# A graph layer on one core: GpSimd waits for landed rows at every half tile, two context chunks behind the chain, feed-forward weights loaded later

## The chip, the cores and the metric

The kernel runs on one core of one Trainium2 chip. The time is the device time of one execution, in microseconds (us); lower is better. TensorE is called PE in the profile, VectorE DVE, ScalarE ACT, GpSimd POOL and SyncE SP.

## The reference

The input is a table `x` of 6250 nodes with 256 channels, and 106,250 edges (source, target), sorted by target. Every node is normalized (layer norm) to `xn`. Then three things are computed and added up:

```python
# graph attention, 4 heads of 64 channels
h = (xn @ W).reshape(-1, 4, 64)
e = leaky_relu(a_src[src] + a_dst[dst], 0.2)      # a_src, a_dst: h times a vector per head
ex = exp(e - segment_max(e, dst)[dst])
alpha = ex / segment_sum(ex, dst)[dst]
gat = sigmoid(segment_sum(alpha * h[src], dst) + bias)
# linear attention over all nodes, 8 heads, with a gate
q, k, v = split(xn @ Wqkv); k = softmax(k, axis=nodes)
context = einsum(k, v); out = q @ context
mix = (out * sigmoid(gelu(ln(xn) @ Wg1 + bg1) @ Wg2 + bg2)) @ Wproj + bproj
x = x + gat + mix
# feed-forward on the nodes that a top-k of a router weight selects
y = (gelu(ln(x) @ w1 + b1) @ w2 + b2) * weight    # zero where not selected
x = x + y + ln(x)
```

## The kernel before, in words

Nodes are cut in 49 tiles of 128 rows (`NT`), edges in 52 tiles of 2048 (`NI`). Every engine has its own program; the programs meet at semaphores. The program has a setup block, a block for a fallback that isn't entered with these inputs, the main block, and a short last block that writes the result.

The **setup block** (from L250) loads all of `x`, takes the means and variances (DVE, `stats`, L427), forms the inverse root (L483 to L503), multiplies every node tile by the weights (PE, L674 and L680) and stores per node a row of 260 numbers (`feat_d`, 256 channels and the source scores) and smaller rows of target scores (`adst_d`). DVE moves the products out of PE's accumulator (`evacuate`, L514 to L530), SP stores them (L302). In between GpSimd and DVE prepare the edge lists: DVE casts them to float (L462), GpSimd works on them (L354 to L406). SP also loads the two feed-forward weights there (L330, 1 MB each), into space that the edge lists held until then.

The **main block** handles edge tile k in these stages. GpSimd fetches the source rows: 16 indirect DMAs (`gather`, L737) of 128 rows each, in 4 groups of 4 (`fill`). They land in `ring`, which has a slot for even k and one for odd k, and each group counts up a semaphore of its own (`rows_in{u}{g}`, u the slot, g the group). A group of tile k may only be issued once PE has summed the half of tile k-2 that held its place (`sums_done`). The scores of the edges go PE (L1552), DVE (L1178 to L1198), PE (turned, L1568), DVE (two scans that form the running maxima, L1206 and L1209), PE (turned back, L1577), DVE (L1218, L1222), ACT (exponentials, L1425). Then DVE scales the gathered rows (L1235, one operation per group) and PE sums them by target (L1610, 8 products a group), and ACT copies each half's sums out (L1444), after which GpSimd may reuse that half.

The other work of a step belongs to node tiles some steps behind: merging the sums (5 behind), the linear attention's products and the gate (6 behind; PE L1531, L1539, L1621; ACT L1455; DVE L1135), the feed-forward's first product (7 behind, L1638, GELU on ACT L1472) and its second (L1589, taken out by DVE L1228, 8 behind). `steps(engine, list)` lays the stages of one step out in the order of the list, for every engine apart, so the lists in the last lines of each engine's program set the order. Steps 0 to 9 and the last ones are written out, the others are a loop of two steps.

The **context** of the linear attention sums over all nodes, so it must be done before the first merge. It is cut in 10 chunks (`CHUNKS`): chunk 0 stands ahead of step 0, and the steps 0 to 4 hold the other nine. Each needs loads of `x` by SP (L1055), DVE, ACT (L1406, L1414) and PE (L1488).

```python
        CONTEXT_A = lambda f: (0, 5, lambda k, u: f(2 * k + 1, u))
        CONTEXT_B = lambda f: (0, 4, lambda k, u: f(2 * k + 2, u))
                        pool.wait_ge(S("idx_made"), 2)
```

`known_below(k, n)` is true where k is a constant under n; `number` turns a step's number into what the engine compares with. `sweep` is a loop over tiles with a body of `n` tiles.

## Time and profile before

| | us |
|---|---|
| median of 3 runs | 2220.82 (2220.32 to 2227.02) |
| the profiled execution's own time | 2227.13 |
| its span, first to last instruction | 2225.3 |
| PE busy | 1179.6 |
| DVE busy | 1046.6 |
| POOL busy | 835.9 |
| ACT busy | 570.4 |
| mean granted TensorE clock | 0.71 |

The span is what the trace covers. Busy is the time in which an engine executed; time in which it waited for a semaphore or issued a DMA is not in it. No engine is busy for much more than half of the span, so what matters is which wait ends last in each stretch. In the rows further down, the idle time of an engine ahead of an instruction stands in brackets with what released it: an engine, a value and a line, or `issue`, which is time in which the engine waited for nothing that the profile shows, or `remote`, a wait whose releaser can't be named from the records.

### The profile page before, as it was taken

To read this page: it belongs to the slowest core of one execution; us is meant where nothing else is said; L and a number is where in the kernel's file an instruction comes from. 1 tells how busy PE (TensorE), PEld (TensorE's weight loads), DVE (VectorE), ACT (ScalarE), POOL (GpSimd) and SP (SyncE) were. 2 spreads that over 40 slices of the span, in tenths; PEclk is the share of its full clock that TensorE was granted. 3 is DMA by queue.
4 is the path that set the end of the run, shared out by engine and by line. 5 is a ranking of instruction groups with operands and counts; after the bars stand their busy time and mean duration, and the time that the engine had idled before them with its cause. 6 is when DMAs were issued, how large, how long until landed. Compare 5 with 4: busy or idle time off the path is not lost. (4 is left out here: it accounts for less than half of the span.)

```text
span 2225.3 us, 26752 instructions
## 1 busy us (share of the span) xinstructions
PE 1179.6 (53%) x6583; PEld 925.9 (42%) x6583; DVE 1046.6 (47%) x2649; ACT 570.4 (26%) x1372; POOL 835.9 (38%) x881
## 2 busy tenths in 40 slices
PE   4975344544545455454545464646363636364682
PEld 3753223323434444343434353535352525343571
DVE  7543334353544444444535353535353535353557
ACT  3432211111222222222222222313131313131360
POOL 4002342444434343535353535353434343444200
PEclk7987666666767676767677667667667767676795
DMA  6566342333333332323232323232323333333203
GB/s 172 184 165 169 96 114 81 87 99 100 89 82 91 78 94 75 98 71 97 72 100 71 103 66 103 71 98 76 93 74 95 79 95 78 93 85 86 70 22 116
DMA packets 166018, 210.85 MB, mean 95 GB/s; under 512 B 51163, under 2 KB 130587, under 8 KB 165871
## 3 DMA queue, kind: packets, MB, share of 16 engines
q0 software_dynamic: 39984, 110.94, 19.7%
q1 hardware_dynamic: 125991, 99.41, 15.8%
q8 instruction: 18, 0.29, 0.1%
q14 instruction: 25, 0.20, 0.0%
HBM read 165.93 MB, written 44.30 MB: 94 GB/s over the span
## 5 line engine op out<-in xcount | busy, mean ns | idle before, releaser
L737 POOL DMA_INDIRECT ring<-feat_d,idx x832 | 801.1, 963 | 1122.0 <-issue 569.6
L1638 PE MATMUL bank<-late,w_s 128*128 128x128 f32 x1568 | 312.9, 382 | 659.9 <-ACT late L1465 659.9
L1638 PEld LDWEIGHTS bank<-late,w_s 128*128 128x128 f32 x1568 | 304.6, 293 | 690.1 <-issue 630.6
L1228 DVE TENSOR_TENSOR big<-bank,b2row 128x256 f32 (+1 forms) x49 | 20.8, 424 | 592.2 <-remote 592.0
L1610 PE MATMUL bank<-ring,hot 128*64 128x265 f32 x1664 | 217.7, 414 | 49.0 <-DVE ring L1235 45.1
L1235 DVE TENSOR_TENSOR ring<-ring,bank 128x1024 f32<-128x1024 f32 x208 | 240.0, 1217 | 1.8 <-ACT bank L1425 1.8
L1455 ACT ACTIVATE sc<-bank,hbg 128x128 f32<-128x128 f32 x98 | 30.6, 363 | 816.9 <-remote 806.2
L1589 PE MATMUL bank<-w_s,hT 128*128 128x256 f32 x784 | 185.9, 390 | 3.7 <-ACT hT L1472 3.7
L1610 PEld LDWEIGHTS bank<-ring,hot 128*64 128x64 f32 x1664 | 125.4, 145 | 124.0 <-issue 68.3
L1589 PEld LDWEIGHTS bank<-w_s,hT 128*128 128x128 f32 x784 | 146.9, 193 | 22.7 <-ACT hT L1472 4.3
L1472 ACT ACTIVATE hT<-bank,b_s 128x128 f32<-128x128 f32 x392 | 110.3, 372 | 44.8 <-PE bank L1638 44.2
L1488 PE MATMUL bank<-big,sc 128*128 (+1 forms) x196 | 71.2, 516 | 89.3 <-issue 43.3
L1488 PEld LDWEIGHTS bank<-big,sc 128*128 128x128 f32 x196 | 45.9, 252 | 112.1 <-issue 95.5
L1568 PE MATMUL bank<-ident,lk 128*16 128x128 f32 x208 | 37.9, 299 | 100.6 <-issue 68.0
L1425 ACT ACTIVATE bank<-diff 128x64 f32<-128x64 f32 x52 | 11.8, 228 | 305.6 <-DVE diff L1222 298.5
L1621 PE MATMUL bank<-wproj_s,sc 128*128 128x256 f32 x196 | 86.2, 585 | 0.0
L1444 ACT ACTIVATE wout<-bank 128x265 f32<-128x265 f32 x104 | 40.7, 392 | 169.8 <-PE bank L1610 167.7
L1089 DVE TENSOR_TENSOR late<-late,big 128x256 f32<-128x256 f32 x49 | 20.8, 425 | 118.0 <-ACT big L1406 59.8
L1218 DVE TENSOR_TENSOR ring<-bank,lastT 128x64 f32<-128x64 f32 x52 | 11.7, 225 | 119.7 <-PE bank L1577 106.3
L674 PE MATMUL bank<-late,xnT 128*128 128x328 f32 x196 | 66.5, 464 | 0.6 <-ACT xnT L592 0.6
L1206 DVE TENSOR_TENSOR_SCAN forth<-brk,bank 16x512 f32<-16x512 f32 x52 | 62.5, 1202 | 8.9 <-PE bank L1568 6.2
L1153 DVE TENSOR_TENSOR hot<-bank,dlocT 128x512 f32<-128x512 f32 x104 | 66.5, 680 | 0.0
(249 smaller groups left out, 1729.8 us busy)
## 6 DMA issues: line engine op xcount, KB each, us to landing
parts_d<-wout SPq DMA_DIRECT2D x208, 66.2 KB
ring<-feat_d,idx POOLq DMA_INDIRECT x832
lists<-dloc_d SPq DMA_DIRECT2D x104, 128.0 KB
parts_d<-hot SPq DMA_DIRECT2D x50, 265.0 KB
parts<-parts_d SPq DMA_DIRECT2D x49, 265.0 KB
xs<-in_x SPq DMA_DIRECT2D x74, 128.0 KB
feat_d<-parts SPq DMA_DIRECT2D x49, 130.0 KB, 2.9
big<-in_x SPq DMA_DIRECT2D x7, 896.0 KB, 10.8
```

What stands on the lines that cost most here:

```text
L674: mm = T.matmul(bank[2 + u][:, 0:WA], tile[:, t * P:(t + 1) * P], wa_s[:, t, :], start=(t == 0), stop=(t == CT - 1))
L737: pool.indirect_dma_start(out=ring[:, u * TI + q, 0:AW], out_offset=None, in_=feat_d, in_offset=bass.IndirectOffsetOnAxis(ap=idx[:, u, q:q ...
L1153: V.tensor_tensor(hot[:, tiles, :], iota_ps.unsqueeze(1).to_broadcast([P, 2 * TG, WIN]), dlocT[:, bass.ds(k, 1), tiles].rearrange("p a q - ...
L1206: V.tensor_tensor_scan(forth[:, :], brk[:, 0:GE], bk_t[0:TI, :], LOWEST, ALU.add, ALU.max).then_inc(S("forth_made"), 1)
L1235: V.tensor_tensor(feats, feats, ex[:, g * TG:(g + 1) * TG, :].unsqueeze(3) .to_broadcast([P, TG, HEADS, HD]), ALU.mult).then_inc(S("scaled ...
L1444: A.activation(wout[:, n, :], bank[2 + n][:, 0:SW], ACT.Copy).then_inc(S("sums_kept"), 1)
L1472: A.activation(hT[:, m, :], bank[6 + m // 4][:, (m % 4) * P:(m % 4 + 1) * P], ACT.Gelu_apprx_tanh, bias=b1_s[:, m:m + 1]).then_inc(S("gelu ...
L1488: mm = T.matmul(bk_c[t][:, 0:C], sc[:, u, t * P:(t + 1) * P], big[:, bass.ds(i, 1), :].rearrange("p a c -> p (a c)"), start=s, stop=e)
L1589: mm = T.matmul(bk_o[:, 0:C], hT[:, m, :], w2_s[:, m, :], start=(m == 0), stop=(m == FT - 1))
L1610: mm = T.matmul(bank[2 + n][c * WIN:(c + 1) * WIN, 0:SW], hot[:, q, :], ring[:, u * TI + q, 0:SW], start=(j == 0), stop=(j == TG - 1))
L1621: mm = T.matmul(bk_t[:, 0:C], sc[:, u, t * P:(t + 1) * P], wproj_s[:, t, :], start=(t == 0), stop=(t == CT - 1))
L1638: mm = T.matmul(bank[6 + m // 4][:, (m % 4) * P:(m % 4 + 1) * P], w1_s[:, t, m * P:(m + 1) * P], xn2T[:, t * P:(t + 1) * P], start=(t == 0 ...
```

## The change

Four things are changed.

1. GpSimd's `fill` waits for rows to have landed. Ahead of group 2 of a tile it waits until groups 0 and 1 of this tile are there, ahead of group 0 (from tile 1 on) until group 3 of the tile before is there. Four groups make a tile, so there are never more than 8 indirect DMAs under way.
2. The two context stages of a step stand together, late in the step, on SP, DVE, ACT and PE; before, one of them stood at the head of the step. Each engine's list has one entry fewer.
3. SP loads the two feed-forward weights at the head of the main block, ahead of `steps`, instead of in the setup block, whose end then doesn't wait for them. PE waits for them ahead of its first feed-forward product.
4. DVE casts the edge lists behind the first four `evacuate`, instead of between two parts of the statistics.

```diff
@@ setup block, SP @@
                 store_targets(1)
-                sp.wait_ge(S("lists_turned"), 6)
-                sp.wait_ge(S("order_checked"), 1)
-                for o, i in later:
-                    sp.dma_start(o, i).then_inc(S("ffn_in"), 16)
                 sweep(sp, TARGETS[2], NT, 0, 0, store)
...
-                sp.wait_ge(S("ffn_in"), 32)
@@ setup block, DVE @@
                 stats(4)
-                dve.wait_ge(S("edges_in"), 32)
-                for n, to in enumerate((ed_dst, ed_src)):
-                    V.tensor_copy(to, ed_i[:, (1 - n) * IE:(2 - n) * IE]).then_inc(S("edges_float"), 1)
                 stats(5)
...
-                sweep(dve, 0, STOPS[1], 2, 0, evacuate)
+                for i in range(4):
+                    evacuate(i, i % 2)
+                dve.wait_ge(S("edges_in"), 32)
+                for n, to in enumerate((ed_dst, ed_src)):
+                    V.tensor_copy(to, ed_i[:, (1 - n) * IE:(2 - n) * IE]).then_inc(S("edges_float"), 1)
+                sweep(dve, 4, STOPS[1], 0, 0, evacuate)
@@ the context's place @@
-        CONTEXT_A = lambda f: (0, 5, lambda k, u: f(2 * k + 1, u))
-        CONTEXT_B = lambda f: (0, 4, lambda k, u: f(2 * k + 2, u))
+
+        def CONTEXT(f):
+
+            def two(k, u):
+                for n in range(2 * k + 1, min(2 * k + 3, len(CHUNKS))):
+                    f(n, u)
+
+            return 0, 5, two
+
@@ main block, GpSimd @@
-                        made, used = number(pool, k + 1), None
+                        made, used, landed = number(pool, k + 1), None, None
                         if not known_below(k, 2):
                             used = number(pool, NB * (k - 2) + g // 2 + 1)
+                        if g == 2:
+                            landed = (f"rows_in{u}{g - 1}", number(pool, 32 * (k - u) + 64))
+                        elif g == 0 and not known_below(k, 1):
+                            landed = (f"rows_in{1 - u}{GI - 1}", number(pool, 32 * (k - 1 - (1 - u)) + 64))
                         pool.wait_ge(S("idx_made"), 2)
                         if g == 0:
                             pool.wait_ge(S("idx_made"), made)
+                        if landed is not None:
+                            pool.wait_ge(S(landed[0]), landed[1])
                         if used is not None:
                             pool.wait_ge(S("sums_done"), used)
@@ main block, SP @@
+                for o, i in later:
+                    sp.dma_start(o, i).then_inc(S("ffn_in"), 16)
+
-                steps(sp, [CONTEXT_A(context), AHEAD(ahead), MERGE(load_x), CONTEXT_B(context), AHEAD(breaks_ahead),
+                steps(sp, [AHEAD(ahead), MERGE(load_x), CONTEXT(context), AHEAD(breaks_ahead),
                            EDGES(windows), NODE_AHEAD(load_node)])
@@ main block, PE @@
                 def first_ff1(i, u):
                     pe.wait_ge(S("xn2T_kept"), i + 1)
+                    if known_below(i, 1):
+                        pe.wait_ge(S("ffn_in"), 32)
                     ff1_half(i, 0)
...
-                steps(pe, [CONTEXT_A(context), EDGES(turn_scores), FF1(first_ff1), EDGES(turn_maxima), SUM(project), FF1(other_ff1),
-                           EDGES(first_sums), EDGES(other_sums), AHEAD(scores_ahead), CONTEXT_B(context), FF1(ff2),
+                steps(pe, [EDGES(turn_scores), FF1(first_ff1), EDGES(turn_maxima), SUM(project), FF1(other_ff1),
+                           EDGES(first_sums), EDGES(other_sums), AHEAD(scores_ahead), CONTEXT(context), FF1(ff2),
                            FOLD(fold), MERGE(mixer), SUM(turn_normed), SEARCH(search)])
```

The lists of DVE and ACT change in the same way. What this makes of the order is shown at three places. The line numbers of the changed kernel differ a little (L737 is L734 there).

GpSimd, tile 1's last group and tile 2's first three. A row with a wait is the first gather of a group, "x3" the other three. Before:

```order
L737 DMA ring<-feat_d,idx 128x260 [waits idx_made]
L737 DMA ring<-feat_d,idx 128x260 x3
L737 DMA ring<-feat_d,idx 128x260 [waits sums_done,idx_made]
L737 DMA ring<-feat_d,idx 128x260 x3
L737 DMA ring<-feat_d,idx 128x260 [waits sums_done,idx_made]
L737 DMA ring<-feat_d,idx 128x260 x3
L737 DMA ring<-feat_d,idx 128x260 [waits sums_done,idx_made]
```

And of the change:

```order
L734 DMA ring<-feat_d,idx 128x260 [waits idx_made]
L734 DMA ring<-feat_d,idx 128x260 x3
L734 DMA ring<-feat_d,idx 128x260 [waits rows_in13,sums_done,idx_made]
L734 DMA ring<-feat_d,idx 128x260 x3
L734 DMA ring<-feat_d,idx 128x260 [waits sums_done,idx_made]
L734 DMA ring<-feat_d,idx 128x260 x3
L734 DMA ring<-feat_d,idx 128x260 [waits sums_done,rows_in01,idx_made]
```

Every other group has one more wait. No gather has moved.

SP's queue at the head of the main block: the loads of `x` for context chunks (L1055, L1065), two weights, then the target scores (`stat`) for the next edge tile. Before:

```order
L1004 DMA brk<-brk_d 16x512
L1055 DMA xs<-in_x 128x256 [waits renormed] x2
L1055 DMA sa<-in_x 128x256 [waits renormed] x2
L1069 DMA hT<-in_L0_mix_Wqkv 128x2x256
L1070 DMA parts<-in_L0_mix_Wqkv 128x2x256
L1055 DMA xs<-in_x 128x256 [waits renormed] x2
L1055 DMA sa<-in_x 128x256 [waits renormed] x2
L975 TENSOR_LOAD base_i
L998 ISA
L998 DMA stat<-adst_d 64x12
```

And of the change:

```order
L1014 DMA brk<-brk_d 16x512
L1065 DMA xs<-in_x 128x256 [waits renormed] x2
L1065 DMA sa<-in_x 128x256 [waits renormed] x2
L1079 DMA hT<-in_L0_mix_Wqkv 128x2x256
L1080 DMA parts<-in_L0_mix_Wqkv 128x2x256
L1084 DMA w1_s<-in_L0_ffn_w1 128x2x1024
L1084 DMA w2_s<-in_L0_ffn_w2 128x8x256
L985 TENSOR_LOAD base_i
L1008 ISA
L1008 DMA stat<-adst_d 64x12
```

The two weights (1 MB each) stand where the loads for chunk 1 stood, and those loads come behind the target scores.

PE, the start of step 0. `stat` and `lists` give the edges' scores, `sc` and `big` are the context's factors, `lk` the scores, `srow` the maxima. Before:

```order
L1552 MATMUL bank<-stat,lists 128x24 x7
L57 UNCONDITIONAL_BRANCH
L57 ISA
L1488 ISA [waits renormed,keys_exp]
L1488 MATMUL bank<-big,sc 128x256 x2
L1484 REGISTER_ALU
L1488 ISA [waits renormed,keys_exp]
L1488 MATMUL bank<-big,sc 128x256 x2
L57 REGISTER_ALU
L57 COMPARE_AND_BRANCH
L1568 MATMUL bank<-ident,lk 16x128 [waits leaky_made]
L1568 MATMUL bank<-ident,lk 16x128 x3
```

And of the change:

```order
L1565 MATMUL bank<-stat,lists 128x24 x7
L1581 MATMUL bank<-ident,lk 16x128 [waits leaky_made]
L1581 MATMUL bank<-ident,lk 16x128 x3
L1590 MATMUL bank<-ident,srow 128x16 [waits max_made,idx_made]
L1590 MATMUL bank<-ident,srow 128x16 x3
L1623 MATMUL bank<-ring,hot 64x265 [waits hot_made,ex_made,scaled,maxcol_made,lastcol_made]
```

The context chunk's products have left the place ahead of the step's chain; they follow behind the scores of the next tile.

## Rows read from the trace of the kernel before

**Rows 1.** The page's busy times of the engines, whole span.

```profile
PE 1179.6 (53%) x6583; PEld 925.9 (42%) x6583; DVE 1046.6 (47%) x2649; ACT 570.4 (26%) x1372; POOL 835.9 (38%) x881
```

**Rows 2.** The page's costliest groups: busy, mean ns of one, idle before and its releaser.

```profile
L737 POOL DMA_INDIRECT ring<-feat_d,idx x832 | 801.1, 963 | 1122.0 <-issue 569.6
...
L1228 DVE TENSOR_TENSOR big<-bank,b2row 128x256 f32 (+1 forms) x49 | 20.8, 424 | 592.2 <-remote 592.0
...
L1455 ACT ACTIVATE sc<-bank,hbg 128x128 f32<-128x128 f32 x98 | 30.6, 363 | 816.9 <-remote 806.2
```

**Rows 3.** Timeline of one loop step: start, duration (us), engine, line, operation, [idle before].

```profile
1002.22 0.94 POOL L737 DMA_INDIRECT ring<-feat_d,idx  x1 [17.45 <-issue]
...
1003.13 3.70 PE L1589 MATMUL bank<-w_s,hT 128*128 128x256 f32 x16
...
1007.65 0.71 PE L1539 MATMUL bank<-hidT,wg_s 64*128 64x128 f32 x4
...
1010.15 0.61 PE L1568 MATMUL bank<-ident,lk 128*16 128x128 f32 x4 [1.42 <-issue]
...
1021.30 0.95 POOL L737 DMA_INDIRECT ring<-feat_d,idx  x1 [0.30 <-issue]
1025.52 0.42 DVE L1228 TENSOR_TENSOR big<-bank,b2row 128x256 f32 x1 [15.43 <-remote]
1025.57 0.62 ACT L1455 ACTIVATE sc<-bank,hbg 128x128 f32<-128x128 f32 x2 [18.89 <-remote]
...
1030.61 0.66 PE L1577 MATMUL bank<-ident,srow 16*128 16x16 f32 x4
...
1031.40 0.23 DVE L1218 TENSOR_TENSOR ring<-bank,lastT 128x64 f32<-128x64 f32 x1 [2.39 <-PE bank L1577]
...
1032.36 4.62 DVE L1235 TENSOR_TENSOR ring<-ring,bank 128x1024 f32<-128x1024 f32 x4
...
1036.59 3.80 PE L1610 MATMUL bank<-ring,hot 128*64 128x265 f32 x32
...
1038.79 0.39 ACT L1444 ACTIVATE wout<-bank 128x265 f32<-128x265 f32 x1 [0.94 <-PE bank L1610]
...
1039.62 0.95 POOL L737 DMA_INDIRECT ring<-feat_d,idx  x1 [17.38 <-PE bank L1610]
```

**Rows 4.** DMA engines' busy tenths in 40 slices, window 1023.5 to 1024.5 us.

```profile
DMA  8800400000000000000000000000000000000000
```

**Rows 5.** Group of L1218 from 600 to 2000 us: first and last start.

```profile
L1218 DVE TENSOR_TENSOR ring<-bank,lastT x38: 224/226/226, 628.1 to 1984.6; 128x64 f32<-128x64 f32 x38
```

**Rows 6.** Timeline of the setup block where the feed-forward weights load.

```profile
170.43 1.36 SPq L330 DMA_DIRECT2D w_s<-in_L_ffn_w  x2
...
187.06 0.49 DVE L514 TENSOR_SCALAR parts<-bank,rstd 128x260 f32<-128x260 f32 x1 [14.09 <-DMA feat_d<-parts]
```

**Rows 7.** Timeline of the setup block around casts and the inverse root.

```profile
28.02 2.35 DVE L462 CAST w_s<-ring 52x2048 f32<-52x2048 int32 x2
...
40.37 5.37 POOL L360 TENSOR_SCALAR ring<-ring 52x2047 f32<-52x2047 f32 x1
...
40.66 3.41 DVE L489 TENSOR_TENSOR xs<-rstd 128x49 f32<-128x49 f32 x1
...
52.65 0.36 DVE L489 TENSOR_TENSOR xs<-rstd 128x49 f32<-128x49 f32 x1
```

**Rows 8.** Timeline of the main phase's first steps, GpSimd and ScalarE.

```profile
205.23 0.95 POOL L737 DMA_INDIRECT ring<-feat_d,idx  x1 [41.15 <-POOLq L760]
...
244.43 0.95 POOL L737 DMA_INDIRECT ring<-feat_d,idx  x1 [0.30 <-issue]
...
250.55 0.60 ACT L1414 ACTIVATE sc<-xs,rstd_neg,rstd 128x256 f32<-128x256 f32 x1 [9.06 <-remote]
...
273.50 0.95 POOL L737 DMA_INDIRECT ring<-feat_d,idx  x1 [28.13 <-PE bank L1610]
...
312.40 0.94 POOL L737 DMA_INDIRECT ring<-feat_d,idx  x1 [18.61 <-PE bank L1610]
```

More of the change, by code:

```diff
@@ L1396, in _ @@
                 context(0, 0)
-                steps(dve, [CONTEXT_A(context), EDGES(target_scores), EDGES(edge_hots), EDGES(scores), OUT(outputs),
+                steps(dve, [EDGES(target_scores), EDGES(edge_hots), EDGES(scores), OUT(outputs),
                             SUM(products), EDGES(maxima), EDGES(differences), MERGE(merge_weights), EDGES(messages), AHEAD(hots_ahead),
-                            CONTEXT_B(context), SUM(sums), MERGE(merge), SUM(normed), FOLD(fold), SEARCH(search)])
+                            CONTEXT(context), SUM(sums), MERGE(merge), SUM(normed), FOLD(fold), SEARCH(search)])
             @block.scalar
@@ L1476, in _ @@
                 context(0, 0)
-                steps(act, [CONTEXT_A(context), EDGES(exps), MERGE(merge_exp), GELU(hidden), EDGES(keep_sums), CONTEXT_B(context),
+                steps(act, [EDGES(exps), MERGE(merge_exp), GELU(hidden), EDGES(keep_sums), CONTEXT(context),
                             SUM(inverse_root), MERGE(gates), SUM(keep_turned)])
```

## The prediction

> **What bounds the kernel now.** I read the page first. GpSimd's 832 gathers fill only 801.1 us of a 2225.3 us span; PE is the busiest engine with 53% [rows 1, 2]. So nothing is at its limit, and I looked at the waits. Two groups stand out: DVE's L1228 is preceded by 592.2 us of idle time and ACT's L1455 by 816.9 us, nearly all of it "remote" [rows 2]. Both wait for a product of PE in every step.
>
> The timeline of one loop step shows why [rows 3]. The step goes from the first gather at 1002.22 to the next tile's first gather at 1039.62: 37.4 us. The gathers start at 1002.22 and follow each other by 1.27 us; the sixteenth starts at 1021.30 and ends at 1022.25, so the train takes 20.0 us. PE's L1589 is finished at 1003.13 + 3.70 = 1006.83, and its reader L1228 starts at 1025.52. PE's L1539 is finished at 1007.65 + 0.71 = 1008.36, and its reader L1455 starts at 1025.57. Both readers start together, 17 to 19 us after their inputs were ready and 3.3 us after the last gather's end. DVE itself can't be the reason: before L1228 it idled 15.43 us; nor ACT, which idled 18.89. My reading: **what PE reports is held while GpSimd issues gathers, and comes out some 3.3 us after the train**. L1568, the turned scores, ended at 1010.76 and is read only behind L1228.
>
> After the release comes the chain that GpSimd waits for: from L1228 (1025.52) 5.09 us to L1577, 0.79 to L1218, 0.96 to L1235 (4.62 us for four groups), the sums L1610, their copy L1444 at 1038.79, and 0.83 us later the next gather. Release to next train: 14.1 us. Train start to release: 23.3. A step is the sum of these two, since the train of tile k+2 needs the sums of tile k and these need the release behind the train of tile k+1. L1218 starts at 628.1 and, 37 intervals later, at 1984.6: 36.66 us a step in the mean [rows 5].
>
> **The waits for landed rows.** They add two pauses to a step, one in the middle and one ahead of the next tile. How long does GpSimd pause? Around the end of a train the DMA engines work until the slice that ends at 1023.63 at most [rows 4] (the fifth slice of 0.025 us behind 1023.5), some 1.4 us after the last gather's end at 1022.25. A restart on a semaphore takes up to 0.83 us, as after L1444 [rows 3]. Landing (1.4, up to 1.7 with the semaphore itself) plus restart: 2.2 to 2.5 us; I take 2.5. Ahead of a tile this costs nothing, for there GpSimd waits 17.38 us for the sums [rows 3]; rows landed long before. In the middle it counts: the train becomes two halves of 7 x 1.27 + 0.95 = 9.85 us with 2.5 us between them, 22.2 us instead of 20.0.
>
> The Trainium skill, "DMA: Bandwidth & Descriptors", section "Anatomy of one DMA — SWDGE (gpsimd) path", gives such a DMA a fixed cost of about 2.0 us, most of it the confirmation that the last byte has landed, ahead of the semaphore. By it a middle pause would be some 0.5 us longer than by the row, 52 x 0.5 = 26 us in the sum; it speaks against a wait for landing, as this change adds one.
>
> What the pause may give back: if what PE reports is let out when GpSimd stands still with nothing under way, the products of the first half step (L1589, L1539, L1568) reach their readers about 3.0 us after the first half, at 9.85 + 3.0 = 12.9 us from the train's start, not at 23.3. DVE and ACT then do L1228, L1455 and the scans during the second half. L1577 follows 5.1 us later, at 18.0: that lies inside the second half (12.4 to 22.2), so its report is held again until 22.2 + 3.3 = 25.5. Then L1218 at once; L1235 0.96 later, two groups of it 2.3; 16 of the sums' products 1.9 (half of 3.80); copy and restart 0.9. Next train at 25.5 + 0.96 + 2.3 + 1.9 + 0.9 = 31.6, 31.7 with rounding up of the parts. Before, PE was busy with a product of the feed-forward when L1235's first groups were ready (L1610 starts at 1036.59, 4.2 us after L1235); that product now lies earlier. Against the mean of 36.7 this is 5.0 us a step. Steps 8 to 51 are 44: **-220 us**. Bounds: from -11.6 a step (no hold left, below) to +2.5 a step (no release in the pause).
>
> **The weights' load.** In the setup, SP issues the two loads of 1 MB at 170.43, and the `feat_d` stores behind them come late: DVE waits 14.09 us for such a store before its evacuation at 187.06 [rows 6]. This goes: -14. In the main block the loads stand ahead of the target scores of tile 1, where only chunk 1's loads stood. There their 2 MB take the time that they took in the setup, 12 to 14 us, and what covers it is step 0, whose gathers alone run 39 us [rows 8]; if that cover is gone, +12, once. I take 0.
>
> **The casts.** They take 2.35 us [rows 7], and GpSimd's preparation of lists starts with them. In before it runs beside DVE's inverse root: L489 takes 3.41 us beside GpSimd's L360 and 0.36 us without it. The root's chain has five such stretches, together some 8.5 us, an estimate from this pair. The change runs the root alone, but puts the casts (2.35) and the slow stretches among the first evacuations, where DVE has slack. I take -4, half of it; bounds -8.5 and +2.4.
>
> The Trainium skill, "SBUF — State Buffer", section "SBUF: two separate sides", says that a DVE operation with two inputs in SBUF and a GpSimd operation lock each other out; by this rule, the trace agrees, with 3.41 against 0.36 us.
>
> **The context behind the chain.** The first train is of two tiles, 32 gathers from 205.23 to 245.38 [rows 8]; ACT's next context operation starts at 250.55, after 9.06 us of "remote", 5.2 us behind the train. Steps 1 and following take 38.9 us there (273.50 to 312.40). The order now lets the edge tile's chain go first, and chunk loads wait less in the way of the scores. The five steps could each win up to the chunk's products and the wait ahead of them, some 8 us, as much as the 9.06 us wait; and with the pauses above the steps 0 to 7 gain like the loop. But the context must be done before the first merge, and its two chunks a step remain. I take -30 for steps 0 to 7 in all; bounds 0 and -58 (8 x 7.3).
>
> **Sum.** 2227.13 - 220 - 14 - 4 - 30 = 1959 us for an execution like the profiled one. Its own time lies 6.3 us over the median of the runs, so I forecast 1950 (rounded from 1953).
>
> **Rivals.**
>
> *B: no hold at all with at most 8 gathers under way.* If the hold needs a long train (it shows itself behind 16 and 32 gathers; nothing shows 8), all of PE's reports come promptly. Then a step is bounded by GpSimd: 2 x (9.85 + 2.5) and 0.4 for small pauses, 25.1 us, since the chain of 14.1 us and the 8.5 us ahead of it (1002.22 to 1010.76) are 22.6 together. 44 x (25.1 - 36.7) = -510; 2227 - 510 - 48 = 1669, to 1750 if half of the second half's hold is left. For it: reports that end before the train aren't held. Against: L1539 was finished 6 us into the train, with 5 gathers issued, and was held already.
>
> *C: slower.* The release came 3.3 us after the last gather, the pause lasts only 2.5. If what lets reports out is the end of work that runs on for 3.3 us (5.2 behind 32 gathers, so it grows with the train), the second half begins before anything has been let out, and the hold runs through both halves. Then nothing is gained and every tile pays the 2.5 us: 52 x 2.5 = +130, less the 18 of the setup: 2227 + 130 - 18 = 2339, or 2300 with the context's gain. The point from which it decides: whether the tail behind 8 gathers is shorter than 2.5 us. Going from 5.2 for 32 to 3.3 for 16, 8 would leave 2.3, just under it. That makes this the strongest rival.
>
> *D: the release in the pause happens, but wins little,* since the chain's end stays behind the second half and ACT and DVE have other work there: -1 to -2 us a step, 2100 to 2200.
>
> *E: the waits find the rows landed, no pause, no gain.* Against: a group's last gather is issued 0.3 us ahead of the wait, its rows land 1.4 us later [rows 3, 4]. Only setup and context would count then, and if they also come to nothing, it is the same.
>
> **Chances.** Forecast 0.50, own range 1830 to 2090 (-3 to -9 us a step). B 0.12. D 0.08. E with nothing 0.03. C 0.27. So faster by over 0.3% 0.70, within 0.3% 0.03, slower 0.27; 0.3% (7 us) is about what a measurement of this kernel can tell from no change. The range goes from 1780, which leaves B out with its 0.12, to 2330, which takes C's likely end in and leaves its tail.
>
> **What would show it.** Right: L737's idle time grows by about 52 middle pauses of 2.5 us, L1228 and L1455 start in or just behind the pause, about 12.9 us after a tile's first gather, their remote waits fall below 400 us, and L1218 comes every 31 to 32 us. B: L1577 is read within 1 us and the pitch is 25 us. C: L1228 starts 25 to 26 us after the first gather, and the pitch of L1218 is 39. Setup: the 14.09 us wait is gone, the main block starts some 18 us earlier. Wrong I would be above all if the release isn't tied to gathers under way, but to something that a pause of 2.5 us doesn't touch.

## The result and the profile after

The changed kernel takes **1705.53 us** (median of 4 runs, 1688.08 to 1724.12) against 2223.7 us for the kernel before in the same set of runs (2220.32 to 2227.02): a ratio of 0.7644, 95% interval 0.7579 to 0.7708. It takes 23.6% less time there. The prediction was 1950 us with a range of 1780 to 2330, so the time lies below the range. The profiled execution of the changed kernel took 1724.12 us, 1.1% over the median; it counts as a slow one and is left out of the ratio, which is that of the means of the others.

And this is only half of the result. On three other chips the kernel before took not 2223 but 1413 to 1415 us, and there the same change makes it 20.7% slower. The experiments below show both.

These rows of the changed kernel's page answer to [rows 1] and [rows 2] (busy time and share, then busy, mean ns of one, idle before and its releaser):

```profile
PE 1185.9 (69%) x6583; PEld 921.9 (54%) x6583; DVE 1041.1 (60%) x2649; ACT 569.1 (33%) x1372; POOL 847.6 (49%) x881
...
L734 POOL DMA_INDIRECT ring<-feat_d,idx x832 | 811.8, 976 | 631.1 <-issue 453.4
...
L1468 ACT ACTIVATE sc<-bank,hbg 128x128 f32<-128x128 f32 x98 | 30.5, 362 | 306.5 <-remote 293.5
...
L1241 DVE TENSOR_TENSOR big<-bank,b2row 128x256 f32 (+1 forms) x49 | 20.7, 423 | 113.2 <-remote 112.3
```

L1228 is L1241 now, L1455 is L1468. The remote wait of the one has gone from 592.0 to 112.3 us, of the other from 806.2 to 293.5. GpSimd's idle time has gone from 1122.0 to 631.1.

One step in the loop, as in [rows 3] (start, duration, engine, line, idle before):

```profile
1008.48 1.15 POOL L734 DMA_INDIRECT ring<-feat_d,idx  x1 [4.21 <-issue]
...
1009.85 3.70 PE L1602 MATMUL bank<-w_s,hT 128*128 128x256 f32 x16
...
1014.38 0.71 PE L1552 MATMUL bank<-hidT,wg_s 64*128 64x128 f32 x4
...
1017.65 0.95 POOL L734 DMA_INDIRECT ring<-feat_d,idx  x1 [0.30 <-issue]
...
1020.47 0.42 DVE L1241 TENSOR_TENSOR big<-bank,b2row 128x256 f32 x1 [3.69 <-remote]
1020.52 0.62 ACT L1468 ACTIVATE sc<-bank,hbg 128x128 f32<-128x128 f32 x2 [7.12 <-remote]
...
1021.39 0.94 POOL L734 DMA_INDIRECT ring<-feat_d,idx  x1 [2.79 <-issue]
...
1025.56 0.66 PE L1590 MATMUL bank<-ident,srow 16*128 16x16 f32 x4
...
1030.13 0.95 POOL L734 DMA_INDIRECT ring<-feat_d,idx  x1 [0.30 <-issue]
1030.28 0.23 DVE L1231 TENSOR_TENSOR ring<-bank,lastT 128x64 f32<-128x64 f32 x1 [6.32 <-remote]
...
1037.40 0.98 POOL L734 DMA_INDIRECT ring<-feat_d,idx  x1 [6.32 <-PE bank L1623]
```

The first half of the tile begins at 1008.48. L1602 and L1552 are finished at 1013.55 and 1015.09, and their readers start at 1020.47 and 1020.52: 12.0 us after the first gather and 1.9 us after the eighth ended (1018.60), while GpSimd pauses. The pause is 2.79 us long. L1590 is finished at 1026.22, when four gathers of the second half have ended, and read at 1030.28: 4.1 us late, but while the train is still running. This step (tile 30) is one of the longer ones, 28.92 us to the next tile's first gather at 1037.40. In tile 42 the second half begins at 1343.29:

```profile
1343.29 0.94 POOL L734 DMA_INDIRECT ring<-feat_d,idx  x1 [2.79 <-issue]
...
1347.38 0.66 PE L1590 MATMUL bank<-ident,srow 16*128 16x16 f32 x4
1348.17 0.23 DVE L1231 TENSOR_TENSOR ring<-bank,lastT 128x64 f32<-128x64 f32 x1 [2.39 <-issue]
...
1355.96 0.94 POOL L734 DMA_INDIRECT ring<-feat_d,idx  x1 [2.96 <-PE bank L1623]
```

Here L1590 is finished at 1348.04, again four gathers into the half, and read at once, at 1348.17. Of the 36 tiles from 12 to 47, 16 are like this one (read within 0.25 us); in the other 20 it is read 0.8 to 5.7 us late, and in 2 of these only when the train has ended. The mean is 19.1 us after the tile's first gather. The 16 steps take 26.1 us in the mean, the 20 others 27.8. The earlier the product was finished, the less it was held: all seven that were finished within 4.52 us of the half's first gather were read at once, the three that came later than 5.0 us were all held.

The pitch of the steps, as in [rows 5]:

```profile
L1231 DVE TENSOR_TENSOR ring<-bank,lastT x22: 224/225/226, 615.4 to 1185.6; 128x64 f32<-128x64 f32 x22
```

(1185.6 - 615.4) / 21 = 27.15 us a step, against 36.66 before. The first gather of all and that of tile 8, from which on the forecast counted its 44 steps:

```profile
186.73 0.95 POOL L734 DMA_INDIRECT ring<-feat_d,idx  x1 [32.39 <-POOLq L757]
...
415.58 0.94 POOL L734 DMA_INDIRECT ring<-feat_d,idx  x1 [2.93 <-issue]
```

The first gather stood at 205.23 before [rows 8], so the setup is 18.5 us shorter. The 1306.7 us from tile 8's first gather to the end of the span, and the 228.9 us between the two, hold the rest of the 503 us: the trace before has its tile 8 at 494.61, which makes 1730.7 and 289.4. So 424 us come from the loop and the end, 60.5 from steps 0 to 7, 18.5 from the setup.

### The profile page after: what moved, and what is told of

Its sections match the earlier page's. It is cut to its first block and busy times, and to the rows that moved or that the text cites. A ratio compares the mean times of both kernels' runs of the same rounds, so it can differ in the third digit from the quotient of the medians.

```text
span 1722.3 us, 26791 instructions
## 1 busy us (share of the span) xinstructions
PE 1185.9 (69%) x6583; PEld 921.9 (54%) x6583; DVE 1041.1 (60%) x2649; ACT 569.1 (33%) x1372; POOL 847.6 (49%) x881
## 5 line engine op out<-in xcount | busy, mean ns | idle before, releaser
L734 POOL DMA_INDIRECT ring<-feat_d,idx x832 | 811.8, 976 | 631.1 <-issue 453.4
L1651 PE MATMUL bank<-late,w_s 128*128 128x128 f32 x1568 | 293.1, 365 | 168.3 <-ACT late L1478 166.2
L1651 PEld LDWEIGHTS bank<-late,w_s 128*128 128x128 f32 x1568 | 284.7, 277 | 189.2 <-issue 175.5
L1623 PE MATMUL bank<-ring,hot 128*64 128x265 f32 x1664 | 253.1, 456 | 97.5 <-issue 52.3
L1623 PEld LDWEIGHTS bank<-ring,hot 128*64 128x64 f32 x1664 | 145.7, 161 | 189.5 <-issue 131.2
L1602 PE MATMUL bank<-w_s,hT 128*128 128x256 f32 x784 | 189.6, 393 | 9.0 <-issue 4.9
L1602 PEld LDWEIGHTS bank<-w_s,hT 128*128 128x128 f32 x784 | 147.8, 194 | 30.4 <-issue 7.4
L1468 ACT ACTIVATE sc<-bank,hbg 128x128 f32<-128x128 f32 x98 | 30.5, 362 | 306.5 <-remote 293.5
L1231 DVE TENSOR_TENSOR ring<-bank,lastT 128x64 f32<-128x64 f32 x52 | 11.7, 225 | 162.8 <-remote 83.7
L1501 PE MATMUL bank<-big,sc 128*128 (+1 forms) x196 | 66.3, 493 | 35.2 <-ACT big L1419 19.3
L1241 DVE TENSOR_TENSOR big<-bank,b2row 128x256 f32 (+1 forms) x49 | 20.7, 423 | 113.2 <-remote 112.3
L1283 DVE TENSOR_SCALAR late<-sd,bn 128x256 f32<-128x256 f32 x49 | 21.1, 431 | 102.1 <-issue 54.2
L1581 PEld LDWEIGHTS bank<-ident,lk 128*16 128x16 f32 x208 | 15.8, 96 | 111.9 <-issue 94.5
L1634 PE MATMUL bank<-wproj_s,sc 128*128 128x256 f32 x196 | 74.3, 515 | 0.0
```

The costliest lines, as they stand in the source:

```text
L734: pool.indirect_dma_start(out=ring[:, u * TI + q, 0:AW], out_offset=None, in_=feat_d, in_offset=bass.IndirectOffsetOnAxis(ap=idx[:, u, q:q ...
L1501: mm = T.matmul(bk_c[t][:, 0:C], sc[:, u, t * P:(t + 1) * P], big[:, bass.ds(i, 1), :].rearrange("p a c -> p (a c)"), start=s, stop=e)
L1581: mm = T.transpose(bk_t[0:TI, :].rearrange("r (e j) -> r j e", j=TG)[:, j, :], lk[:, u, j, :], ident[:, :])
L1602: mm = T.matmul(bk_o[:, 0:C], hT[:, m, :], w2_s[:, m, :], start=(m == 0), stop=(m == FT - 1))
L1623: mm = T.matmul(bank[2 + n][c * WIN:(c + 1) * WIN, 0:SW], hot[:, q, :], ring[:, u * TI + q, 0:SW], start=(j == 0), stop=(j == TG - 1))
L1634: mm = T.matmul(bk_t[:, 0:C], sc[:, u, t * P:(t + 1) * P], wproj_s[:, t, :], start=(t == 0), stop=(t == CT - 1))
```

## The experiments

They ran in five sets, each with the kernel before beside it on the same chip. In four sets, on three chips, the kernel before took 1412.65, 1414.67, 1414.73 and 1415.45 us. In the fourth one in order of time, on another chip, it took 2241.91 us, like the 2223.7 of the result. Nothing lies between. I call the second kind a chip **with the hold**. The expectations of the first set were written before this was known, so they are all made for a kernel before at 2223 us.

### The waits alone, and the change without them (no hold)

e1 is the kernel before with part 1 of the change and nothing else.

```diff
+                        if g == 2:
+                            landed = (f"rows_in{u}{g - 1}", number(pool, 32 * (k - u) + 64))
+                        elif g == 0 and not known_below(k, 1):
+                            landed = (f"rows_in{1 - u}{GI - 1}", number(pool, 32 * (k - 1 - (1 - u)) + 64))
...
+                        if landed is not None:
+                            pool.wait_ge(S(landed[0]), landed[1])
```

> The kernel before with nothing but GpSimd's waits for landed rows. Pause theory (PE's reports are held while gathers are issued without a break, and come out in a pause of some 2 us): nearly the whole gain, 1770 to 1810 us, L1218 every 27 to 28 us in the loop. If setup and context carried it: over 2100 us.

Measured: 1721.17 us, ratio 1.2176 (1.2112 to 1.2240) to the kernel before at 1412.65. The number lies 49 us under the expected range, and it is a loss, not a gain.

e2 is the changed kernel without these lines.

```diff
-                        if g == 2:
-                            landed = (f"rows_in{u}{g - 1}", number(pool, 32 * (k - u) + 64))
-                        elif g == 0 and not known_below(k, 1):
-                            landed = (f"rows_in{1 - u}{GI - 1}", number(pool, 32 * (k - 1 - (1 - u)) + 64))
```

> The changed kernel without its waits for landed rows (other three parts kept). Pause theory: the loop keeps its 36.7 us a step, only setup (-18) and some of the context's steps (up to -30) are gained: 2170 to 2205 us. If the order of context and loads carried the gain: near 1705 us.

Measured: 1391.54 us, ratio 0.9851 (0.9806 to 0.9895). Neither theory had this. The three other parts win 21 us, and the waits cost 314 us (against the change itself, e6, on another chip of the same kind).

### Other spacings (no hold)

e3 waits ahead of every group:

```diff
-                        if g == 2:
+                        if g > 0:
```

> The changed kernel with a wait ahead of every group of 4 gathers. Pause theory: the hold is shorter, but GpSimd's own time is 4 x (3 x 1.25 + 0.95 + 3.0) = 31 us a step, so it becomes the bound: 31 to 32 us a step, 1870 to 1900 us. If fewer gathers under way simply make everything faster: below 1705 us.

Measured: 1949.09 us, ratio 1.3801 (1.3739 to 1.3863), 31.4 us a step as worked out for a GpSimd that is the bound (here 4 pauses of 2.7 to 3.7 us), but in all 49 us over the expected range. The gain that would have paid for it wasn't there to be had.

e4 waits for the group before last only:

```diff
-                        if g == 2:
-                            landed = (f"rows_in{u}{g - 1}", number(pool, 32 * (k - u) + 64))
-                        elif g == 0 and not known_below(k, 1):
-                            landed = (f"rows_in{1 - u}{GI - 1}", number(pool, 32 * (k - 1 - (1 - u)) + 64))
+                        if g > 1:
+                            landed = (f"rows_in{u}{g - 2}", number(pool, 32 * (k - u) + 64))
+                        elif not known_below(k, 1):
+                            landed = (f"rows_in{1 - u}{GI - 2 + g}", number(pool, 32 * (k - 1 - (1 - u)) + 64))
```

> The changed kernel, but a group waits only for the rows of the group before last: never more than 8 gathers under way, as in the change, yet no pause, since those rows land some 1.5 us behind their gather. Pause theory: as without waits, 2170 to 2205 us. If the number under way is what counts: 1640 to 1710 us.

Measured: 1394.20 us, the same as e2 and neither of the two expected. The cap on the gathers under way costs nothing (its trace has 0.30 us ahead of a gather in mid-tile, no pause): it is the standstill that costs.

### The two kernels themselves on such a chip

> The kernel before itself, with a trace. In the runs of the waits alone it took 1412.65 us, where the profiled execution that the prediction reads took 2227. Theory of two modes (the hold of PE's reports is a property of the chip or of how the program sits on it, not of the program): either near 1412 us with L1218 every 20 to 21 us and L1228 within 1 us of PE's product, or near 2223 us with 36.7 us a step, and nothing in between. Theory of a gradual influence (temperature, clock): something in between.

Measured: 1414.81 us, as the theory of two modes says; nothing in between was seen in this set or in any other. Its page (engines, granted clock in tenths of full speed by slices of the span, two groups):

```profile
PE 1064.9 (75%) x6583; PEld 834.2 (59%) x6583; DVE 1052.9 (75%) x2649; ACT 567.6 (40%) x1372; POOL 851.6 (60%) x881
...
PEclk9797968987699999999999999989999998999975
...
L737 POOL DMA_INDIRECT ring<-feat_d,idx x832 | 816.8, 982 | 313.5 <-issue 244.9
...
L1455 ACT ACTIVATE sc<-bank,hbg 128x128 f32<-128x128 f32 x98 | 30.7, 364 | 83.7 <-PE bank L1539 83.7
```

PE is busy for somewhat less than before (1064.9 us against 1179.6 [rows 1], at a higher granted clock), but ACT's L1455 waits 83.7 us in all where it was 806.2 us [rows 2], and the wait has PE's product as its releaser. One step of it:

```profile
899.82 3.70 PE L1589 MATMUL bank<-w_s,hT 128*128 128x256 f32 x16
...
904.35 0.71 PE L1539 MATMUL bank<-hidT,wg_s 64*128 64x128 f32 x4
...
905.09 0.63 ACT L1455 ACTIVATE sc<-bank,hbg 128x128 f32<-128x128 f32 x2 [1.71 <-PE bank L1539]
...
907.74 0.17 DVE L1189 COPY idx<-srcT 128x16 int32 x1 [1.02 <-DMA ring<-feat_d,idx]
...
912.36 0.62 PE L1577 MATMUL bank<-ident,srow 16*128 16x16 f32 x4
...
913.11 0.23 DVE L1218 TENSOR_TENSOR ring<-bank,lastT 128x64 f32<-128x64 f32 x1 [0.90 <-PE bank L1577]
```

L1589 and L1539 lie in the middle of a train of gathers, as in [rows 3], and L1539, finished at 905.06, is read at 905.09. L1577, finished at 912.98, is read at 913.11.

The traces also record when a semaphore counts up. The one that L1539 counts up and ACT waits for does so 17.1 us (median of the 49 node tiles) behind the product's end in the trace before, and 0.01 us behind it in e5. So it is the report that comes late, and not ACT that looks late.

```profile
L1218 DVE TENSOR_TENSOR ring<-bank,lastT x34: 224/225/227, 604.1 to 1281.8; 128x64 f32<-128x64 f32 x34
```

That is (1281.8 - 604.1) / 33 = 20.54 us a step. Sixteen gathers at a pitch of 1.25 take 20.0, so GpSimd is the bound here.

> The changed kernel itself beside the kernel before. If this chip shows no hold: 1690 to 1710 us against 1412, slower by some 20%, since the waits then only cost: each tile pays two landings and restarts. If it shows the hold: 1690 to 1724 against 2223.

Measured: 1705.59 us, ratio 1.2070 (1.2026 to 1.2115). It takes the same time with and without the hold. Its GpSimd and the DVE operation that waits for the rows:

```profile
1009.25 0.94 POOL L734 DMA_INDIRECT ring<-feat_d,idx  x1 [2.78 <-issue]
...
1018.23 0.94 POOL L734 DMA_INDIRECT ring<-feat_d,idx  x1 [0.30 <-issue]
...
1022.24 0.17 DVE L1202 COPY idx<-srcT 128x16 int32 x1 [7.03 <-DMA ring<-feat_d,idx]
...
1023.05 0.94 POOL L734 DMA_INDIRECT ring<-feat_d,idx  x1 [3.88 <-DVE idx L1202]
...
1032.77 0.94 POOL L734 DMA_INDIRECT ring<-feat_d,idx  x1 [0.30 <-issue]
...
1036.46 0.94 POOL L734 DMA_INDIRECT ring<-feat_d,idx  x1 [2.75 <-issue]
```

The second half of one tile runs from 1009.25 to 1019.17 (9.92 us), then comes a pause of 3.88; the first half of the next from 1023.05 to 1033.71 (10.66), and a pause in mid-tile of 2.75, like the one ahead of 1009.25. Together 27.21 us:

```profile
L1231 DVE TENSOR_TENSOR ring<-bank,lastT x22: 224/225/226, 618.3 to 1191.9; 128x64 f32<-128x64 f32 x22
```

(1191.9 - 618.3) / 21 = 27.31 us a step. Nothing but GpSimd's gathers and its pauses is left in the step. The profile names DVE's L1202 as what ended the pause of 3.88, but the indices that this tile needs were made one tile earlier; L1202 itself waits for the same landed rows. It starts at 1022.24, 3.07 us after the last gather's end, and GpSimd restarts 0.81 later. The Trainium skill, "DMA: Bandwidth & Descriptors", section "Anatomy of one DMA — SWDGE (gpsimd) path", gives about 2.0 us for setup and completion together, most of it the wait for the confirmation that the last byte has landed. By that rule, the trace agrees for the pause in mid-tile, 2.78 us with a restart of some 0.8, and shows more for the other, 3.07 without the restart.

### One wait of the two, and a standstill that asks nothing (no hold)

e7 keeps the wait ahead of group 2, e12 that ahead of group 0.

```diff
-                        elif g == 0 and not known_below(k, 1):
-                            landed = (f"rows_in{1 - u}{GI - 1}", number(pool, 32 * (k - 1 - (1 - u)) + 64))
```

> The changed kernel with the wait ahead of group 2 only, not ahead of group 0. Pause theory with hold: the wait ahead of a tile is covered by other waits, so near 1705. Without hold: a tile pays one pause of some 2.8 us and its train runs on into the next, 52 x 2.8 = 146 over 1391, 1530 to 1550 us, if one pause alone is the price of each wait.

Measured: 1510.69 us, ratio 1.0712 (1.0658 to 1.0766), 119 us over e2, 2.3 us a tile, and 19 under the expected range (e7's pauses are 2.7 to 3.1 us, 2.77 in the median, less the 0.30 that lie between any two gathers).

And e12:

```diff
-                        if g == 2:
-                            landed = (f"rows_in{u}{g - 1}", number(pool, 32 * (k - u) + 64))
-                        elif g == 0 and not known_below(k, 1):
+                        if g == 0 and not known_below(k, 1):
```

> The changed kernel with the wait for landed rows ahead of group 0 only. Without hold the two waits add up: e6 minus e7 is 195 us, so 1391.5 + 195 = 1586 us. With hold (kernel before at 2223 on this chip): the train keeps its 16 gathers, the release comes 3.3 us behind it, near e2's time with hold, 2170 to 2230.

Measured: 1545.13 us, ratio 1.0917 (1.0881 to 1.0953), 154 us over e2 and 41 below what was expected. The waits don't add up: 119 + 154 = 273, together they cost 314.

e8 has no wait for rows, but a fill by GpSimd ahead of group 2:

```diff
+        still = sb("still", [P, 2400])
...
-                            landed = (f"rows_in{u}{g - 1}", number(pool, 32 * (k - u) + 64))
-                        elif g == 0 and not known_below(k, 1):
-                            landed = (f"rows_in{1 - u}{GI - 1}", number(pool, 32 * (k - 1 - (1 - u)) + 64))
+                            landed = ("pool_made", number(pool, k + 9))
+                            pool.memset(still[:, :], 0.0).then_inc(S("pool_made"), 1)
```

> The changed kernel without waits for landed rows, but with a fill of 2400 values by GpSimd ahead of group 2 (some 2.4 us by its fills in the setup, of 0.41 us for 384 values and 0.60 for 513), so GpSimd stands still in the middle of a tile without asking whether rows landed. With hold: as e7, since the standstill lets reports out. Without hold: 1391 + 52 x 2.4 = 1516 us.

Measured: 1514.90 us, ratio 1.0711 (1.0665 to 1.0757), like e7. That it meets the 1516 is in part luck: the standstill between two gathers is 3.08 us, 2.12 of it the fill, and 52 x (3.08 - 0.30) would be 145 us, of which 123 came.

### The other three parts, undone one at a time from e2 (no hold)

e2 was run in another set, on the same chip; the kernel before took 1412.65 us there and 1414.73 here, so 2 us of each difference to e2 may be the sets'.

e9 puts back the casts:

```diff
                 stats(4)
+                dve.wait_ge(S("edges_in"), 32)
+                for n, to in enumerate((ed_dst, ed_src)):
+                    V.tensor_copy(to, ed_i[:, (1 - n) * IE:(2 - n) * IE]).then_inc(S("edges_float"), 1)
...
-                for i in range(4):
-                    evacuate(i, i % 2)
-                dve.wait_ge(S("edges_in"), 32)
-                for n, to in enumerate((ed_dst, ed_src)):
-                    V.tensor_copy(to, ed_i[:, (1 - n) * IE:(2 - n) * IE]).then_inc(S("edges_float"), 1)
-                sweep(dve, 4, STOPS[1], 0, 0, evacuate)
+                sweep(dve, 0, STOPS[1], 2, 0, evacuate)
```

> The changed kernel without its waits for landed rows (1391.5 us as e2), with the casts of the edge lists back between the statistics. Prediction's term: the first gather comes 4 us later than in e2 (184.31), bounds 2.4 earlier to 8.5 later: 1389 to 1400 us.

Measured: 1402.95 us, ratio 0.9903 (0.9874 to 0.9932): 11.4 us slower than e2. The first gather of e2 and of e9:

```profile
184.31 0.96 POOL L734 DMA_INDIRECT ring<-feat_d,idx  x1 [30.24 <-POOLq L757]
```

```profile
195.60 0.95 POOL L732 DMA_INDIRECT ring<-feat_d,idx  x1 [31.30 <-POOLq L755]
```

It comes 11.3 us later in these two executions, more than the 8.5 that were the upper bound. But kernels with one and the same setup have their first gather between 182.12 (e3) and 186.73 us (the change), so such a difference is known to some 4 us.

e10 puts back the load of the weights:

```diff
                 store_targets(1)
+                sp.wait_ge(S("lists_turned"), 6)
+                sp.wait_ge(S("order_checked"), 1)
+                for o, i in later:
+                    sp.dma_start(o, i).then_inc(S("ffn_in"), 16)
```

> As e2, with the load of the feed-forward weights back in the setup. Prediction's term: the 14 us wait ahead of one evacuation returns, first gather 14 us later than in e2: 1403 to 1407 us. If another wait had taken its place anyway: 1391.

Measured: 1402.91 us, ratio 0.9921 (0.9890 to 0.9952), 11.4 us slower than e2. The wait of [rows 6] is back, and the first gather:

```profile
175.97 0.49 DVE L511 TENSOR_SCALAR parts<-bank,rstd 128x260 f32<-128x260 f32 x1 [13.76 <-DMA feat_d<-parts]
...
192.59 0.96 POOL L739 DMA_INDIRECT ring<-feat_d,idx  x1 [38.81 <-POOLq L762]
```

It comes 8.3 us later, not 13.8 (again known to some 4 us): part of the wait is covered by what follows.

e11 puts one context stage back at the head of the step, on all four engines:

```diff
-                steps(act, [EDGES(exps), MERGE(merge_exp), GELU(hidden), EDGES(keep_sums), CONTEXT(context),
+                steps(act, [CONTEXT_A(context), EDGES(exps), MERGE(merge_exp), GELU(hidden), EDGES(keep_sums), CONTEXT_B(context),
```

> As e2, with one context stage back at the head of the step. Prediction's term for steps 0 to 7 was 30 us, made in a trace with the hold. Without hold GpSimd is fed better: 0 to 10 us slower than e2, 1391 to 1401 us.

Measured: 1398.65 us, ratio 0.9897 (0.9864 to 0.9930): 7.1 us slower than e2. As expected it is little where nothing is held. One at a time the three parts are worth 11.4, 11.4 and 7.1 us, 29.9 in sum, and together 21; of the 9 us between, up to 6 may be the sets' (2 us each).

### With the hold

In the next set the kernel before took 2241.91 us. All three kernels of it were chosen to answer on either kind of chip. e13 is e2 again, e15 is e8 again, and e14 is e8 with a shorter fill:

```diff
-        still = sb("still", [P, 2400])
+        still = sb("still", [P, 600])
```

> The changed kernel without its waits for landed rows, once more. No hold (kernel before at 1412 us in this set): 1391 us. Hold (kernel before at 2223): 2170 to 2205 us, 36 us a step.

Measured: 2222.44 us, ratio 0.9915 (0.9881 to 0.9949) to the kernel before. That is 17 us over the range, on a chip where the kernel before takes 18 us more than was assumed. The same kernel took 1391.54 as e2. Its steps:

```profile
L1225 DVE TENSOR_TENSOR ring<-bank,lastT x35: 224/226/226, 604.1 to 1867.1; 128x64 f32<-128x64 f32 x35
```

(1867.1 - 604.1) / 34 = 37.15 us, as before. So with the hold the three other parts bring 19 us (11 to 27 by the interval), the setup's share. From the first gather to that of tile 8 e13's trace takes 286.1 us, against 289.4 before and 228.9 in the changed kernel: the 60 us of steps 0 to 7 were the waits' too.

> As e8, with a fill of 600 values (some 0.8 us). No hold: 1391 + 52 x 0.8 = 1433 us, or 1391 if GpSimd has that much slack in a step. Hold: too short to let reports out, which came 1.9 us behind a train of 8, so 2190 to 2250 us.

Measured: 2203.94 us, ratio 0.9849 (0.9740 to 0.9959). The rows of a step:

```profile
1006.01 0.71 PE L1552 MATMUL bank<-hidT,wg_s 64*128 64x128 f32 x4
...
1009.63 0.95 POOL L735 DMA_INDIRECT ring<-feat_d,idx  x1 [0.30 <-issue]
1010.58 0.61 POOL L967 MEMSET still<- 128x600 f32 x1
...
1012.16 0.95 POOL L735 DMA_INDIRECT ring<-feat_d,idx  x1 [0.97 <-issue]
...
1020.92 0.95 POOL L735 DMA_INDIRECT ring<-feat_d,idx  x1 [0.30 <-issue]
...
1024.34 0.62 ACT L1468 ACTIVATE sc<-bank,hbg 128x128 f32<-128x128 f32 x2 [19.29 <-remote]
```

The fill takes 0.61 us. From the end of the eighth gather (1010.58) to the next (1012.16) are 1.58 us. L1552 was finished at 1006.72 and is read at 1024.34, behind the second half. So it is in all 36 tiles from 12 to 47. DVE's L1241 gets its report within the second half in 26 of them, but the rest of the chain waits for the later ones.

> As e8 (1514.9 us there). No hold: 1515. Hold: long enough to let reports out, 1650 to 1750 us, as the change itself.

Measured: 1761.40 us, ratio 0.7872 (0.7751 to 0.7993). It lies 11 us over the range, waits for no rows, and wins what the change wins but for some 3%:

```profile
1005.53 0.71 PE L1552 MATMUL bank<-hidT,wg_s 64*128 64x128 f32 x4
...
1009.67 0.95 POOL L735 DMA_INDIRECT ring<-feat_d,idx  x1 [0.30 <-issue]
1010.60 2.12 POOL L967 MEMSET still<- 128x2400 f32 x1
...
1012.70 0.62 ACT L1468 ACTIVATE sc<-bank,hbg 128x128 f32<-128x128 f32 x2 [8.08 <-remote]
...
1013.69 0.95 POOL L735 DMA_INDIRECT ring<-feat_d,idx  x1 [0.97 <-issue]
```

The eighth gather ends at 1010.62, and L1468 starts at 1012.70, 2.1 us later, with the next gather at 1013.69, 3.07 us after.

```profile
L1231 DVE TENSOR_TENSOR ring<-bank,lastT x39: 224/226/226, 609.1 to 1637.9; 128x64 f32<-128x64 f32 x39
```

(1637.9 - 609.1) / 38 = 27.07 us a step. The same kernel as e8 on a chip without the hold took 1514.90.

### The last set (no hold again)

e16 is e4 again, e17 is e7 again, and e18 is e8 with a fill of 1500 values (`still = sb("still", [P, 1500])`).

> As e4: never more than 8 gathers under way, no standstill. Hold on this chip (before near 2240): if the standstill is what lets reports out, 2200 to 2240 us; if the number under way, near 1750. No hold (before near 1414): 1394.

Measured: 1395.82 us, ratio 0.9864 (0.9835 to 0.9892), as e4. The kernel before took 1415.45 us, so the case with the hold wasn't tried.

> As e7, a wait in mid-tile only. Hold: the wait ahead of a tile is covered by that for the sums, so 1700 to 1760 us as the change and e15. No hold: 1511.

Measured: 1516.00 us, ratio 1.0713 (1.0678 to 1.0747), as e7. The case with the hold wasn't tried here either.

> As e8 with a fill of 1500 values, 1.35 us by the fills of 600 (0.62) and 2400 (2.12). Hold: the reports came 1.9 us behind a train of 8, later than this standstill ends, so near 2200 us. No hold: 1391 + 52 x 1.35 = 1462 us.

Measured: 1500.45 us, ratio 1.0603 (1.0569 to 1.0637), 38 us over what was expected. The fill of 1.37 us is followed by 0.97 us ahead of the next gather, so the standstill is 2.3 us, less 0.3, and 52 x 2.0 = 104 us on 1391.5 make 1496. Where it would stand with the hold isn't known: 2.3 us lies between the 1.58 that don't help and the 3.07 that do, beside the 1.9 to 2.1 us after which reports came.

## Why the prediction was wrong

**The reading of what bounds the kernel was right for the chip that was read.** PE's reports are held while GpSimd issues gathers, and a standstill lets them out: e13, e14 and e15 differ in the length of a standstill alone, and take 2222, 2204 and 1761 us. The number of gathers under way wasn't asked with the hold (e16 fell on a chip without), so that a cap without a standstill does nothing there stays argued, not shown.

**The pause.** 2.5 us were forecast; it was 2.79 in the step shown, 2.99 in the mean. The release was forecast 12.9 us after a tile's first gather, and came after 12.0. The tail behind 8 gathers was to be 2.3 by extrapolation and decide between the forecast and rival C; it was 2.0 in the median. These steps hold.

**The step that failed: "its report is held again until 22.2 + 3.3 = 25.5".** L1590's report is read 19.1 us after the tile's first gather in the mean, not 25.5: at once in 16 of 36 tiles, and in 18 of the others before the train's last gather had ended. I had taken it from [rows 3] that a report that falls in a train waits for its end, but there the reports came from early in a train of 16 and nothing showed one from the second half of a tile behind a pause. With this term at 19.1 the chain's sum gives 25.2 us a step in place of 31.6, and then it no longer sets the step in every tile: two halves of 9.9 and two pauses of 3.0 make 25.8. Where the report came at once a step takes 26.1, where it was held the chain still ends last (27.8, and 28.92 in tile 30); the mean measured is 27.15. Against 36.66 this is -9.5, not -5.0 a step: 44 x 9.5 = 418 us of the 424 measured from tile 8 on. Why a report from the first half is held for 5 to 7 us and one from the second half often not at all stays open.

**Rival B** had the bound that came, two halves and two pauses at 25.1 us, and its 1669 to 1750 us contain the 1705.53. But its condition, no hold with at most 8 gathers under way, isn't met: in the first half L1552's report was held till the pause in 35 of 36 tiles.

**The same 1705 us with the hold and without is in part luck.** Without it (e6) GpSimd's pauses fill every step, 2.8 and 3.9 us in the mean. With it they are 3.0 and 4.1 us, but the second is 2.8 to 3.4 us in 25 of 39 tiles and up to 8.9 where the chain ends last.

**Where the wait ahead of a tile was costed at nothing,** its cover was the 17.38 us for the sums. In the changed kernel that cover has gone down (6.32 us ahead of 1037.40) and in most tiles is hardly longer than the wait for the rows (2.96 ahead of 1355.96), and without the hold it is gone altogether: then this wait costs 154 us alone (e12).

**Steps 0 to 7.** -30 was forecast, -60.5 came. The order of the context isn't what brought it: e13 has it and gains nothing beyond the setup. The waits shorten these steps as they do the loop's.

**The setup.** -18 was forecast and -18.5 came, but by luck, of two errors that cancel: the weights' load is worth 8 to 11 us and not 14 (e10), the casts some 11 and not 4 (e9), each known to some 4 us. That GpSimd holds back DVE's inverse root more than the one pair of L489 told, and that the slow operations which move to the evacuations cost little, would explain it, but no run separates them.

**Rival C** is near to what e14 shows: a standstill shorter than the tail lets little out. But it costs nothing there, since GpSimd has its 16 us of other waits in every step, where the rival charged 2.5 us a tile; the change's own pause was longer than the tail. A slowdown came true, though, by another door that no rival had: that PE's reports might not be held at all, even in the kernel before. Then the pauses buy nothing, and all their cost (6.0 us a tile) is paid: +20.7%. The prediction took a property of one set of executions for a property of the program. One trace couldn't show this. The hint was in [rows 1] and [rows 2]: a kernel without an engine above 53%, with a wait that the profile could put on nobody.

**What stays open:** why some chips hold PE's reports. The program is the same, a gather takes the same 0.95 us with the same pitch on both, and the setup is within 2 us. No run here tells whether it is the chip, what else runs near it, or how the program was placed. Nor does any tell whether the profiler has a part in it: each execution on record has a span and a granted clock from its records, and none was timed without. The traces with the hold lack about half of the records of semaphores counting up: 15,306 in the trace before against 32,361 in e5, for the same program and the same 166,000 DMA packets. Whether these records are lost because of the hold or have to do with its cause wasn't asked; a run without the profiler would be the first thing to try.

The fastest kernel where nothing is held is e2, 1391.54 against 1412.65 and 1705.59; with the hold it is the change itself, 1705.53 against 2223.7 and e13's 2222.44. No version that was run is best on both; one standstill in mid-tile costs 7% without the hold (e8) and wins 21% with it (e15).

## What to carry to other kernels

When a reader starts long after its input was finished, and always just behind a train of instructions of another engine, test it by a standstill in that train of a length that you choose: fills of 0.6 and 2.1 us told more here than the sums. A fix that pays for such a wait with pauses on a third engine is worth only as much as the wait, so time both kernels on more than one chip before it is kept. And look at many steps, not at one: the step shown here is held for 4.1 us, and nearly half of the others aren't held at all. A step made of one engine's work and its pauses is a floor that is easily worked out; set it beside the chain's length first, and the measured pauses (2.8 and 3.9 us here for waiting for landed rows and starting again) into it.

## What the runs showed of the hardware that was not expected

- The same program took 1412 to 1415 us on three chips, and 2242 us on a fourth and 2223 in the set of the result, without anything between. In the slow kind PE's semaphore reports that fall in a train of back-to-back indirect DMAs of GpSimd can reach DVE and ACT late (17.2 us after L1539's end in [rows 3]); in the fast kind L1539 is read within 0.1 us.
- The reports of the first half come out 1.7 to 2.5 us after the eighth and last gather of a short train (changed kernel and e15), and 3.1 to 3.8 us after the last of 16 (kernel before and e13). A gap of 1.58 us between gathers is too short for most of them, 2.8 or more is enough.
- A report from the second half, 2.4 to 5.6 us into 8 gathers, was read at once in 16 of 36 tiles of the changed kernel and in 22 of 39 in e15; the others waited 0.4 to 7.4 us.
- SP's issues are slower in the same trains: four L998 took 6.16 us at 1019.64 in the trace before, and 2.50 at 907.29 in e5, without the hold.
- The granted clock of TensorE goes with it: 0.71 in the slow kernel before, 0.88 in the same kernel without the hold, 0.79 to 0.81 in the changed kernel on both. Of its two levels, 1.2 and 2.4 GHz, PE had more of the upper one where its waits were short.
